# An attention and FFN kernel on one core: the FFN down product turned round, in reduced-width float32

## The reference

```
att = einsum(q, k) * scale; y = einsum(att, v); x = y @ Wproj.T + bproj + x      # 12 times
x = layernorm(x_in + attention(x_in))
gate = x @ wg.T; up = x @ wu.T          # wg, wu: int32 weights / 127, 384 x 128
h = silu(gate) * up                     # 384 wide
x = layernorm(x + h @ wd.T)             # wd: int32 weights / 127, 128 x 384
```

## Time and profile before

| what | value |
|---|---|
| median of three runs | 310.0 us |
| the profiled execution's own time | 311.0 us |
| its span, first to last instruction | 309.2 us |
| mean granted TensorE clock | 0.995 of 2.4 GHz |
| busy: PE, DVE, ACT, POOL | 301.6 us (98%), 231.4 us (75%), 195.5 us (63%), 135.4 us (44%) |
| chain that ended last: share of PE, of DVE | 94%, 3% |
| start of the first gate product of chunk 0 | 250.38 us |

### The profile page before, as it was taken

The page is one execution under the profiler, slowest core; times in us unless marked ns, Lnnn a source line. Parts: engine busy times, 40 slices in busy tenths (PEclk is TensorE's granted clock), DMA queues, the critical chain, the costliest instruction groups (busy, mean ns, idle before and its releaser), DMA issues.

```text
span 309.2 us, 9625 instructions
## 1 busy us (share of the span) xinstructions
PE 301.6 (98%) x3962; PEld 281.5 (91%) x3962; DVE 231.4 (75%) x710; ACT 195.5 (63%) x481; POOL 135.4 (44%) x140
## 2 busy tenths in 40 slices
PE   8999999999999999999999999999999999999991
PEld 8989999899998998999989999899998889999991
DVE  0378687786877879768788687787876988888873
ACT  2449768587585774966849668587595374445540
POOL 3037154372553633725227154370556445565441
PEclk9999999999999999999999999999999999999998
DMA  7703011030020300303003020020000000211112
GB/s 265 263 2 112 6 53 61 4 112 2 14 103 2 117 0 4 112 2 106 11 2 115 3 59 22 5 81 0 4 0 4 1 3 10 60 34 35 36 34 72
DMA packets 8908, 14.96 MB, mean 48 GB/s; under 512 B 800, under 2 KB 5280, under 8 KB 8864
## 3 DMA queue, kind: packets, MB, share of 16 engines
q1 hardware_dynamic: 8144, 13.34, 13.2%
q10 hardware_dynamic: 720, 0.99, 0.9%
HBM read 12.23 MB, written 2.10 MB: 46 GB/s over the span
## 4 chain that ended last, share of the span: by engine, by line
PE 94%; DVE 3%; DMA 1%; issue 0%; POOLq 0%; POOL 0%; ACT 0%; DVEq 0%
PE ps L1118 14%; PE ps L986 13%; PE ps L1063 8%; PE ps L1237 7%; PE ps L943 6%; PE ps L944 6%; PE ps L942 6%; PE ps L1031 5%; PE ps L1005 4%; PE ps L1225 4%; PE ps L1226 4%; PE ps L1055 3%; PE ps L959 3%; PE ps L1197 2%; PE ps L997 2%; PE ps L1042 1%
## 5 line engine op out<-in xcount | busy, mean ns | idle before, releaser
L464 POOL TENSOR_TENSOR step_lo<-step,step_hi 128x512 fp32r<-128x512 f32 (+1 forms) x44 | 52.1, 1217 | 41.6 <-ACT step_hi L572 41.6
L427 POOL TENSOR_TENSOR wq_lo<-w,wq_hi 128x512 fp32r<-128x512 f32 x12 | 15.3, 1275 | 88.5 <-ACT wq_hi L549 88.5
L942 PE MATMUL ps<-state_hi,step_hi 128*128 128x258 f32 x165 | 47.4, 288 | 0.0
L944 PE MATMUL ps<-state_hi,step_lo 128*128 128x258 f32 x165 | 46.7, 283 | 0.0
L943 PE MATMUL ps<-state_lo,step_hi 128*128 128x258 f32 x165 | 46.6, 283 | 0.0
L986 PE MATMUL ps<-w,gram 128*128 128x128 f32 x352 | 42.8, 275 | 0.0
L986 PEld LDWEIGHTS ps<-w,gram 128*128 128x128 f32 x352 | 41.1, 192 | 0.0
L545 ACT COPY gk<-ps 128x512 f32<-128x512 f32 x48 | 28.1, 586 | 19.8 <-PE ps L986 19.8
L1118 PE MATMUL ps<-step,gram 128*128 128x128 f32 x320 | 38.7, 279 | 0.0
L1118 PEld LDWEIGHTS ps<-step,gram 128*128 128x128 f32 x320 | 36.8, 191 | 0.8
L592 ACT COPY gram<-ps 128x256 f32<-128x256 f32 x88 | 32.8, 373 | 4.7
(11 more groups left out here) (150 smaller groups left out, 665.0 us busy)
## 6 DMA issues: line engine op xcount, KB each, us to landing
w<-weights SPq DMA_DIRECT2D x12, 592.5 KB, 3.8
xchan<-x_chan SPq DMA_DIRECT2D x8, 256.0 KB, 4.2
out<-xchan SPq DMA_DIRECT2D x7, 256.0 KB, 2.3
xt<-x_tok SPq DMA_DIRECT2D x4, 258.0 KB, 5.2
xt<-x_tok ACTq DMA_DIRECT2D x3, 258.0 KB, 5.6
fw_int<-ffn_weights SPq DMA_DIRECT2D x1, 576.0 KB, 4.9
cst<-consts SPq DMA_DIRECT2D x1, 147.5 KB, 6.6
xt<-x_tok SPq DMA_DIRECT2D x1, 129.0 KB, 2.6
```

The source lines that it names most:

```text
L464: nc.gpsimd.tensor_tensor(split_group(step_lo, g), split_group(step, g), split_group(step_hi_f, g), ALU.subtract).then_inc(step_lo_ready, 1)
L942: nc.tensor.matmul(dst, l_hi, r_hi, start=True, stop=False)
L944: return nc.tensor.matmul(dst, l_lo, r_hi, start=False, stop=True)
```

## The change

The down product of chunks 0 to 6 is turned. The down weights, now kept as fp32r integers in `wgu_hi[:, 768:1152]`, are the stationary operand, and the hidden values the moving one, split in `hid_hi` (a copy by ACT) and `hid_lo` (a subtraction: blocks 0 and 1 on POOL, block 2 on DVE). That is 3 + 3 fp32r matmuls of 512 columns, with channels on the partitions of the result; ACT copies it to SBUF, and 4 f32 matmuls of 128 columns against `project` (identity minus 1/128) turn it back and take off the mean. Both scalings are moved into the hidden values (`SCALE_HID`). The last chunk keeps the old down product.

All of this is laid into the next chunk: the high products stand between gate 0 and gate 1, the low ones between gate 1 and gate 2, z of chunk n+2 at the chunk's head, transposes inside gate 2. `y_part` and `norm2` run two chunks behind. `h1` has four buffers in place of two. The centring of x is gone: `z_stage` reads `xchan` itself, and the mean enters through `nu_means`. In the layers the search for the largest low part is 1152 wide, not 768, and moves from layer 5 to layer 6; the down weights get an fp32r copy (ACT) and a low part (POOL) in layer 3. The loops of the branch not taken are written out.

```diff
-LOW_LAYER = 5
+LOW_LAYER = 6
+SCALE_HID = SCALE_W * SCALE_W
+H1_BUFS = 4
...
+        y = kdiag
+        sq = s_rows
...
 # POOL
-            def chunk(c, slot, ahead=4):
-                if ahead >= 2:
-                    pool.wait_ge(h1_ready, (c + 1) * CT + CT)
-                    rstd1_part(c + 2)
-                if ahead > 0:
-                    norm2(c)
-                if ahead >= 4:
-                    pool.wait_ge(z_done, c + 3)
-                    centre(c + 4, slot)
+            def hid_low(n, j):
+                pool.wait_ge(hid_hi_ready, n * HC + (j + 1))
+                nc.gpsimd.tensor_tensor(hid_lo[:, n % 2, j, :], hid[:, j, :], hid_hi[:, n % 2, j, :].bitcast(F32),
+                                        ALU.subtract).then_inc(hid_lo_first_ready, 1)
+            def chunk(c):
+                if 1 <= c < CHUNKS - 1:
+                    pool.wait_ge(h1_ready, c * CT + CT)
+                    rstd1_part(c + 1)
+                if c >= 1:
+                    hid_low(c - 1, 1)
+                if c >= 2:
+                    norm2(c - 2)
+                if c < CHUNKS - 1:
+                    hid_low(c, 0)
...
+            norm2(CHUNKS - 2)
...
 # ACT
             def ht_copy(n):
                 act.wait_ge(ht_done, n + 1)
+                if n:
+                    act.wait_ge(up_done, n * HC)
                 nc.scalar.copy(ht_hi[:, :], ps[:, HT_BANK, :]).then_inc(ht_hi_ready, 1)
...
                 if c:
                     gate(c, 1)
+                if not last:
+                    hid_high(c, 0)
+                if c:
+                    down_copy(c - 1)
                 gate(c, 2)
                 if not last:
                     ht_copy(c + 1)
+                    hid_high(c, 1)
+                    hid_high(c, 2)
...
 # DVE
+            def hid_low_last(n):
+                j = HC - 1
+                dve.wait_ge(hid_hi_ready, n * HC + (j + 1))
+                nc.vector.tensor_tensor(hid_lo[:, n % 2, j, :], hid[:, j, :], hid_hi[:, n % 2, j, :].bitcast(F32),
+                                        ALU.subtract).then_inc(hid_lo_last_ready, 1)
...
+            def chunk(c):
+                if c:
+                    ht_part(c)
+                if c >= 2:
+                    y_part(c - 2)
+                    var2_part(c - 2)
+                if c:
+                    hid_low_last(c - 1)
+                hid_part(c, 0)
+                if c < CHUNKS - 2:
+                    z_part(c + 2, c + 2, c % 2)
+                hid_part(c, 1)
+                if c < CHUNKS - 2:
                     dve.wait_ge(rstd1_ready, c + 2)
+                    var1_part(c + 2, c % 2)
+                hid_part(c, 2)
...
+            y_part(CHUNKS - 2)
+            var2_part(CHUNKS - 2)
...
 # PE
+            def down_t_high(n, low):
+                out = ps[:, DOWN_BANK, :]
                 pe.wait_ge(y_ready, n + 1)
+                for j in range(HC):
+                    pe.wait_ge(hid_hi_ready, n * HC + (j + 1))
+                    nc.tensor.matmul(out, of_down(wgu_hi, j), hid_hi[:, n % 2, j, :], start=j == 0, stop=False)
...
+            def down_back_stage(n):
+                pe.wait_ge(down_t_ready, n + 1)
+                for t in range(CT):
+                    last = nc.tensor.matmul(ps[:, DOWN_BANK, P * t:P * (t + 1)], down_t[:, P * t:P * (t + 1)], project,
+                                            start=True, stop=True)
+                last.then_inc(down_done, 1)
```

More of the change, by code:

```diff
@@ L355, in z_bank @@
         def z_bank(n, t):
-            return Z_FIRST_BANKS[t // 2] if isinstance(n, int) and n == 0 else Z_BANK
+            return Z_FIRST_BANKS[t // 2] if n == 0 else Z_BANK
         def by_group(part):
@@ L647, in _ @@
             for c in range(CHUNKS):
-                chunk(c, c % 2, last=c == CHUNKS - 1)
+                chunk(c)
             t = CT - 1
@@ L917, in _ @@
             for c in range(CHUNKS):
-                chunk(c, c % 2, CHUNKS - 1 - c)
-            last_slot, parts = 1, [range(CT)[part] for part in halves]
+                chunk(c)
+            y_part(CHUNKS - 2)
+            var2_part(CHUNKS - 2)
+            last_slot, parts = (CHUNKS - 1) % H1_BUFS, [range(CT)[part] for part in halves]
             for h in range(2):
@@ L1227, in gate_stage, with of_down, down_t_low, last_down_stage @@
                             .then_inc(done, 1)
-            def down_stage(n, last_chunk=False):
+            def of_down(part, j):
+                return part[:, 2 * HIDDEN + P * j:2 * HIDDEN + P * (j + 1)]
+            def down_t_high(n, low):
+                out = ps[:, DOWN_BANK, :]
                 pe.wait_ge(y_ready, n + 1)
+                for j in range(HC):
+                    pe.wait_ge(hid_hi_ready, n * HC + (j + 1))
+                    nc.tensor.matmul(out, of_down(wgu_hi, j), hid_hi[:, n % 2, j, :], start=j == 0, stop=False)
+                    if low:
+                        nc.tensor.matmul(out, of_down(wgu_lo, j), hid_hi[:, n % 2, j, :], start=False, stop=False)
+            def down_t_low(n):
+                for j in range(HC):
+                    if j < HC - 1:
+                        pe.wait_ge(hid_lo_first_ready, (HC - 1) * n + j + 1)
+                    else:
+                        pe.wait_ge(hid_lo_last_ready, n + 1)
+                    last = nc.tensor.matmul(ps[:, DOWN_BANK, :], of_down(wgu_hi, j), hid_lo[:, n % 2, j, :],
+                                            start=False, stop=j == HC - 1)
+                last.then_inc(down_t_done, 1)
+            def down_back_stage(n):
[4 more added lines that the diff above has]
+                last.then_inc(down_done, 1)
+            def last_down_stage():
+                n = CHUNKS - 1
                 def products_of(j, tokens, first=(), final=()):
@@ L1266, in _ @@
             a_stage(2)
[L1268 to L1270 removed]
+            z_stage(1, range(CT // 2))
+            ht_stage(0)
+            z_stage(1, range(CT // 2, CT))
             pe.wait_ge(a_ready, 2)
@@ L1277, in _, with chunk @@
             pe.wait_ge(nub_ready, 2)
[L1279 to L1291 removed]
+            def chunk(c, low):
+                spread = not low and c == 0
+                if 1 <= c < CHUNKS - 2:
+                    pe.wait_ge(z_ready, c + 2)
+                    z_stage(c + 2)
+                pe.wait_ge(ht_lo_ready, c + 1)
+                gate_stage(c, 0, low, spread)
+                if c:
+                    down_t_high(c - 1, low)
+                gate_stage(c, 1, low, spread)
+                if c:
+                    down_t_low(c - 1)
+                else:
+                    pe.wait_ge(z_ready, c + 2)
+                    z_stage(c + 2)
+                gate_stage(c, 2, low, spread, parts=(0,))
+                if 1 <= c < CHUNKS - 1:
+                    ht_stage(c + 1)
+                gate_stage(c, 2, low, spread, parts=(1,))
+                if c:
+                    down_back_stage(c - 1)
+                else:
+                    ht_stage(c + 1)
+                if c == CHUNKS - 1:
+                    last_down_stage()
             def chunks(low):
@@ L1296, in chunks @@
                     pe.wait_ge(a_ready, GROUPS)
-                    with loop(pe, CHUNKS // 2 - 1) as i:
-                        for s in range(2):
-                            chunk(i * 2 + s, s, low)
-                for c in range(CHUNKS - 2 if low else 0, CHUNKS):
-                    chunk(c, c % 2, low, CHUNKS - 1 - c)
+                for c in range(CHUNKS):
+                    chunk(c, low)
             with nc.If(low_part[0] == 0):
```

186 lines of the change are left out of this document (80 added, 106 removed).

## The result

The changed kernel takes 318.7 us (median of 4 runs, 317.1 to 320.3) against 310.3, a ratio of 1.027 with a 95% interval of 1.024 to 1.031: slower; the forecast was 317.7. In the profiled executions the span went from 309.2 to 317.2 us.

| stretch | before | after | difference | forecast |
|---|---|---|---|---|
| to chunk 0's first gate | 250.38 | 249.65 | -0.7 | 0 |
| chunk 0's to chunk 7's first gate | 46.7 | 52.9 | +6.1 | +3.6 |
| to the first y half of chunk 7 | 4.74 | 9.37 | +4.6 | +4.4 |
| to the end of ScalarE's last operation | 3.4 | 3.2 | -0.2 | -0.3 |
| to the end of the span | 3.9 | 2.1 | -1.8 | 0 |

What follows compares the result with a forecast made beforehand. PE, busy 98%, bounds the kernel before; DVE was to bound it after. Terms +3.6 (chunks), +4.1 (end), 0 (layers) sum to +7.7: own time 311.0 to 318.7, less 1.0 for the median, 317.7 us; range 312.4 to 320.0.

Steps and rivals of the forecast that it cites:

- DVE becomes the bound through holds: FFN chunks: POOL's subtractions hold a shared SBUF path and DVE's squares wait 1.3 us a chunk; the forecast case, 60%.
- Rival B: FFN chunks: both engines share the path, chunks stay at 6.53 us, total 312.7 to 313.5, within 2%; 30%.
- that term: Chunk 0's to chunk 7's first gate: 50.2 us against 46.6, +3.6 in place of -1.4.
- 7.36 us a chunk: FFN chunk: DVE's queue of 6.06 us plus 1.3 of held squares, with no idle time.
- the layout without holds: FFN queues if nothing slows anything: chunk 0 lasts 6.41 us, PE waiting 1.28 for `ht_lo` of chunk 1; -1.4 us.
- Chunk 7's y half: The end: first y half 9.18 us behind chunk 7's first gate, against 4.74, released by `norm2(6)` and not PE.
- PE's time per chunk: FFN chunk: PE's own work falls to 6.53 us from 6.80, 0.27 less.
- Rival C: FFN chunk: first fp32r product pays 0.08 only behind the old down product; PE saves 0.08 to 0.16 more; 311.6 us; 5%.
- Layers: 0: Layers 5 and 6: moving the search changes the time by between -0.1 and +0.1 us, taken as 0.

Runs made afterwards that it cites:

- Zeros in POOL's place: Changed kernel with GpSimd writing zeros into the low parts of hidden blocks 0 and 1 instead of subtracting: 311.0 us.
- VectorE's order: Changed kernel with VectorE's chunk list reordered, z ahead and both blocks of squares together behind hid 0, own tile for y's squares: 314.95 us.
- the kernel with every remedy: Changed kernel with z-first list, chunk 0 reordered, own tiles for chunk 7's y, var2, rstd2, chunk 6's multiply on ScalarE in four pieces: 311.8 us.
- the copy kernel: Changed kernel with GpSimd copying hidden blocks 0 and 1 into their low parts instead of subtracting: 312.0 us.
- the root freed: Changed kernel with VectorE's low part of the last hidden block moved behind the hid 0 product: 318.57 us.

## Why the prediction was right, and where it was not

- **DVE becomes the bound through holds: right in kind.** Zeros in POOL's place bring the chunk to 6.40, the same work in another order to 6.5, a copy to 6.56. Rival B (meetings are cheap) is refuted, and so is "DVE's own list is too long": it has 0.3 us of room.
- **The size of that term: +3.6 forecast, +6.1 measured.** The step that failed is "7.36 us a chunk" from 1.3 us of held squares. It is 7.66. I let POOL's root of four values run free beside DVE's subtraction, though the earlier trace rows showed such a root lengthened; freed, it gives 0.2 of the 0.3 back. The seven chunks took 52.87 us against 50.24 forecast. Chunks 2 to 5 are 1.2 us of these 2.6; the rest is chunk 1, 8.42 against 6.88, of it 1.2 to 1.4 (an estimate: six or seven products 0.43 and not 0.23 apart) from half the clock behind PE's wait of 2.25 us. No run takes the drop alone out of chunk 1; the nearest pair is VectorE's order with the drop, 7.96, and the kernel with every remedy without it, 6.88. I forecast that wait (1.28 in the layout without holds, chunk 0 at 7.57, measured 7.49) and did not ask what it does to the clock.
- **Chunk 7's y half: 9.18 forecast, 9.37 measured, released by `norm2(6)`.** Right. But with y's buffer, the multiply and the turned product each taken away, 1.0 us more than before stays: the squares of chunks 5, 6 and 7 and their roots fall together there. The end has several causes in a row, and taking one away exposes the next.
- **PE's time per chunk: 6.53 forecast (its own terms add up to 6.55), 6.40 measured.** Rival C was true in substance, not in its condition. Behind the first fp32r product after an f32 one the next starts 0.08 later, but four transposes ahead of fp32r take 0.35 and not 0.43, and the four z products 0.81 and not 0.90 (distances in the timeline of PE of the kernel with the zeros): a switch costs nothing net. It didn't show since DVE was the bound.
- **Missed: the landing of the last output, -1.8 us.** Before, ScalarE's 64 KB took 3.5 us from issue to landing; here 1.7. This does not go with the turned product: x not centred alone on the kernel before has 3.5, and the changed kernel with zeros and the one in VectorE's order 1.7, but the kernel with every remedy has 2.3, and of the two in which chunk 6's product is not turned one has 3.6 and the other 2.3. Its cause is open, and two spans can differ by up to 1.9 us through it.
- **Layers: 0, right, and the measured -0.7 is mostly scatter.** The search takes 1.34 us in layer 6 and 0.95 in layer 5, but it lengthens its layer by less there: from one layer's `mbq` row on DVE to the next layer's it is 19.98 us in place of the usual 19.83, and it was 20.20 before. Layer 5 starts 0.41 us earlier than before and layer 6 0.73, but 0.63 is there in layer 0 already, and the eleven kernels with the changed kernel's layers reach chunk 0's first gate at 249.31 to 250.31, those with the layers of before at 250.12 and 250.38.
- **Net.** In the spans the misses (+2.5, +0.3, -0.7, -1.8) nearly cancelled, 317.2 for 316.9. The other 0.8 us between 317.7 and 318.7 is the step from the profiled execution to the median, taken as 1.0 and measured as 0.2. That was luck: the forecast is better than the working deserved. (The range's lower end, 312.4, is called rival B's, whose own figures end at 312.7.)

The Trainium skill, "SBUF — State Buffer", section "SBUF: two separate sides", has a DVE operation with two SBUF inputs and a GpSimd operation that reads SBUF exclude each other, whichever starts first for its whole length. The trace agrees for the wide operations: the squares at 277.83 and 281.45 and the copy kernel where POOL was first, and POOL's root at 282.90, which waited behind DVE's subtraction of 282.74. It doesn't agree for a root that is first: none here held a square or a subtraction of DVE for its 1.01 us (with the root freed, DVE's subtraction starts its usual 0.60 behind hid 0, 0.45 into the root of 283.18).

## What to carry to other kernels

Before giving work to an idle engine, lay its instruction beside the other engine's queue and ask what each reads: a wide POOL instruction that reads SBUF costs DVE what is left of it when DVE's next instruction has both inputs in SBUF (0.13 to 1.07 us here; a root of four values costs nothing), and moving two subtractions off DVE gained nothing here (7.41 us a chunk with them on DVE, 7.66 with them on POOL). The cheapest remedy is order: let DVE operations that take one input from PSUM stand beside POOL's wide ones (3.8 us here, with no work removed). A step that runs one iteration late still has to be done behind the last one, so price the pipeline's tail before the loop's gain: here the end grew by 4.6 us, against at best seven times 0.4 (6.80 less PE's own 6.40).

## What the runs showed of the hardware

- A POOL write without a read (0.53 us) holds nothing; a copy from SBUF (0.67 us) holds a square for 0.40; a POOL subtraction (1.29) holds one for 0.43 to 1.07; a DVE subtraction (0.68) holds a POOL root for 0.38, and a POOL root holds nothing.
- PE's clock fell to its lower level for about 3.4 us behind waits of 1.88 and 2.25 us, but not behind each such wait and not in each execution of one kernel; in the traces the drop moved from chunk 1 to chunk 6 when the first wait was shortened.
- The landing of a last output of 64 KB took 1.7 us in some kernels and up to 3.6 in others of nearly the same end.
- f32 and fp32r products can alternate on PE at no net cost: the 0.08 us that the fp32r product pays is saved by the f32 one ahead of it.
